# First loads in pieces and products of zeros, weight splits and context units at other places, in a two-layer kernel on one core

## The chip, the cores and the metric

The kernel runs on one core of a Trainium2 chip. Its time is the device time of one execution in microseconds (us), the median of the runs made. PE is TensorE, DVE is VectorE, ACT is ScalarE, POOL is GpSimd, and SP is SyncE, which here only starts transfers.

## What is computed

The input is `x`, 4 x 256 tokens of 256 values (1024 tokens in all), a context of the same shape, and integer token ids. Four blocks add to `x`, each scaled by the tanh of a gate:

```python
# layer 0: one of 4 gated experts, picked by token id, weights (4, 256, 256)
y = einsum(silu(h @ Wg[e].T) * (h @ Wu[e].T), Wd[e]);  out = where(expert_ids == e, y, out)
# layer 0: BitNet feed-forward, ternary weights, 8-bit tokens, Walsh-Hadamard transform before w_down
gate = bitlinear(x, w_gate); up = bitlinear(x, w_up)          # 256 -> 1024
out = h_bitlinear(silu(gate) * up, w_down)                    # act_quant(fwht(.)), 1024 -> 256
# layer 1: cross attention, 16 heads of 128; queries from tokens, keys and values from the context
scores = q @ k.T; out = (softmax(scores) @ v) @ Wo            # batches of 128 queries and 128 keys
# layer 1: 32 experts, top 8 in 2 of 4 groups, latent width 128, plus a shared expert
x = x + tanh(g) * block(layernorm(x))                         # around each of the four
```

`act_quant` takes the largest magnitude `am` of a token, rounds `x * 128 / am` and clips it to -128 .. 127. The layer norms have no weights.

## The kernel before

**Precision.** Weights and activations of the attention are float32. Each is split into a high part (a copy rounded to fp32r) and a low part (the rest), and a product is made of three passes of PE: `hi,lo`, `lo,hi` and `hi,hi` (L1540, L1541, L1542, called through `product`). A high part is written by ACT, a low part by DVE or POOL.

**Context units.** Keys and values of layer 1 come from the context alone, so PE makes them as filler work in units. A unit is six products 128x512 into one PSUM bank: the keys of one head (K) or the values of a group of four heads for one tile of tokens (V), for one half `g` of the tokens. There are 64 (`UNITS`, in the order of `BLOCKS`). `take` on ACT empties the bank, and SP stores the unit to DRAM. The table `FILLS` says how many of them stand at which named place ahead of the attention (`s0`, `s1`, `a11`, `y2`, `u0`, `f0`, ...: 26 in all, `FRONT_UNITS`); the rest stand one each at the places `m0`, `e0`, `m1`, `e1`, ... of the attention loop, m in the middle and e at the end of step u, except those that hold other tasks (`TASK_IN_STEP`).

**Weight blocks.** Weights arrive in 33 blocks of 128x1024 (`BLOCKS`: kind and head group, K, V, Q, O; S, D and E for the last block of the model). SP loads block j into `blk_raw[j % 2]`; `block_high(j)` on ACT (L820) writes the high part, `block_low(j)` on POOL (L574) the low part and counts `blk_done`. A unit of block j waits on PE for `blk_done >= j + 1`. In the attention loop these two calls are the last work of step u on ACT and on POOL, behind the key split of step u+2, for the block that `STEP_OF_BLOCK[u]` names: block 16 in step 7, block 18 in step 9. In the last part of the kernel the expert blocks are split at the units of `UNIT_OF_BLOCK` (ACT) and `LOW_UNIT_OF_BLOCK` (POOL).

**Order.** Each engine runs its own stream in the order of the code. The opening: SP loads context, block 0 and tokens; PE makes three units (`s0`), then transposes the normed tokens (`transpose_norm`, L1554). Then come the products of the four token-id experts for each half g (`a_sel`, masks `ge_row`), and the down products y0. `add_experts` on DVE adds a tile of y0 to `xr`. The BitNet part runs in steps n = 0 .. 7 through the tasks Q (transposes of the rounded tokens), G, U (gate and up), F (transposes of the `fly` product), H (Hadamard), D and C (L1725, L1734, L1740, L1750, L1757, L1763). POOL makes the first levels of the Hadamard transform (`fly`, `inner`, L626 to L632); `quantise` on DVE rounds tokens. Then the attention loop, 32 steps u (16 heads, two halves), and the expert part, 64 units i (32 experts, two halves).

**POOL ahead of the attention.** At the end of the BitNet part POOL runs `key_low(1)` (L580), then waits `h_ready`, then `block_low(7)`, `block_low(8)` and `block_low(9)`. DVE runs there the layer norm of the attention's tokens (L1088, L1089: two operations on 128x4) between operations that H(7) of PE waits for (L1376).

## Time and profile before

| | us |
|---|---|
| median of 3 runs (571.34, 569.83, 569.76) | 569.83 |
| the profiled execution | 570.37 |
| its span in the trace | 568.6 |
| PE busy | 538.2 (95%) |
| DVE, ACT, POOL busy | 389.0, 351.7, 319.9 |
| mean granted clock of TensorE | 0.990 of full |

The span is shorter than the time of the same execution by 1.8 us, which lies around it. A start in the rows below is in us from the span's start. A row of an engine in order of time has start, duration, engine, line of the kernel, operation, what is written from what, and in brackets the idle time ahead of it and who ended it.

### The profile page before, as it was taken

The numbers are of one execution on the slowest core, as the hardware profiler recorded it, in microseconds if no ns is written. First come the engines' busy times: TensorE is split into PE (matmuls) and PEld (weight loads), VectorE is DVE, ScalarE is ACT, GpSimd is POOL, SyncE is SP. The second block draws the span as 40 slices with busy tenths as digits, with TensorE's granted clock in tenths as the row PEclk, the third lists the DMA queues.
The fourth block names the chain that finished last, engine by engine and source line by source line (L and its number), as shares of the span: only waits on it lengthen the run. The fifth ranks groups of instructions, "written<-read, shape, count | busy, mean of one in ns | idle before, by whom it ended". The sixth has DMA issues, their size and how long they took to land.

```text
span 568.6 us, 9604 instructions
## 1 busy us (share of the span) xinstructions
PE 538.2 (95%) x3232; PEld 463.1 (81%) x3232; DVE 389.0 (68%) x818; ACT 351.7 (62%) x723; POOL 319.9 (56%) x318
## 2 busy tenths in 40 slices
PE   3999998998999999999999999999999979999997
PEld 3777766776878989999999999989998868777886
DVE  4867987589956576656655576646665766877882
ACT  3651144566488686766757565745757655777882
POOL 3579037899448797655544424426698464762320
PEclk9999998999999999999999999989999989999999
DMA  9901135610047768677696767534355734546761
GB/s 284 350 22 54 41 109 169 203 39 1 20 164 229 238 189 256 209 254 223 215 288 192 241 210 225 189 105 156 120 191 152 240 121 139 135 143 186 218 181 39
DMA packets 66673, 95.78 MB, mean 168 GB/s; under 512 B 6337, under 2 KB 38849, under 8 KB 66625
## 3 DMA queue, kind: packets, MB, share of 16 engines
q1 hardware_dynamic: 66624, 95.17, 53.6%
q8 instruction: 27, 0.44, 0.3%
q14 instruction: 22, 0.17, 0.1%
HBM read 67.23 MB, written 27.92 MB: 167 GB/s over the span
## 4 chain that ended last, share of the span: by engine, by line
PE 78%; DVE 7%; POOL 5%; ACT 4%; issue 2%; DMA 2%; SPq 0%; DVEq 0%; POOLq 0%; ACTq 0%
PE ps L1540 22%; PE ps L1541 21%; PE ps L1542 21%; PE ps L1645 4%; PE ps L1750 2%; PE ps L1734 2%; DMA xr<-in_x 1%; PE ps L1757 1%; ACT q2T L915 1%; PE ps L1763 1%; POOL kv_w_lo L574 1%; ACT kv_w_hi L820 1%; DMA k_hl<-k_scratch 1%; DVE xr L1194 1%; DVE a_sel L1180 1%
## 5 line engine op out<-in xcount | busy, mean ns | idle before, releaser
L651 POOL TENSOR_TENSOR probs<-probs,rsum 128x512 f32<-128x512 f32 x64 | 66.6, 1043 | 60.4 <-DVE rsum L1246 60.3
L1241 DVE TENSOR_REDUCE nmax<-ps 128x2 f32<-128x512 f32 x64 | 44.0, 688 | 35.6 <-PE ps L1542 35.3
L953 ACT ACTIVATE probs<-ps,nmax 128x256 f32<-128x256 f32 x128 | 59.8, 481 | 1.6 <-DVE nmax L1241 1.4
L1039 ACT ACTIVATE e_hi<-e_r 128x512 fp32r<-128x512 f32 x64 | 40.3, 630 | 31.5 <-DVE e_r L1466 30.4
L574 POOL TENSOR_TENSOR kv_w_lo<-blk_raw,kv_w_hi 128x1024 fp32r<-128x1024 f32 x16 | 38.9, 2434 | 36.2 <-ACT kv_w_hi L820 36.2
L1466 DVE SCALAR_TENSOR_TENSOR e_r<-ps,cw_row 128x512 f32<-128x512 f32 x64 | 43.5, 684 | 14.6 <-PE ps L1542 13.7
L1232 DVE TENSOR_TENSOR pT_lo<-ps,pT_hi 128x512 fp32r<-128x512 f32 x64 | 43.8, 685 | 11.8 <-ACT pT_hi L959 11.2
L1237 DVE TENSOR_TENSOR oT_lo<-ps,oT_hi 128x512 fp32r<-128x512 f32 x32 | 22.1, 692 | 40.1 <-ACT oT_hi L963 40.1
L774 POOL TENSOR_TENSOR e_lo<-e_sq,e_hi 128x512 fp32r<-128x512 f32 x19 | 24.6, 1294 | 43.2 <-ACT e_sq L1045 38.3
L959 ACT ACTIVATE pT_hi<-ps 128x512 fp32r<-128x512 f32 x64 | 38.3, 601 | 15.5 <-PE ps L1645 15.3
L963 ACT ACTIVATE oT_hi<-ps 128x512 fp32r<-128x512 f32 x32 | 19.1, 597 | 40.7 <-PE ps L1542 40.7
L580 POOL TENSOR_TENSOR k_hl<-k_hl 128x512 fp32r<-128x512 f32 x18 | 23.8, 1323 | 31.9 <-ACT k_hl L888 31.9
L1645 PE MATMUL ps<-eye,probs 128*128 128x128 f32 x256 | 39.0, 275 | 1.6 <-DVE kv_out L1272 0.9
L831 ACT ACTIVATE kv_hi<-ps 128x512 fp32r<-128x512 f32 x38 | 22.9, 603 | 26.9 <-PE ps L1542 26.9
L1540 PE MATMUL ps<-pT_hi,v_hl 128*128 128x256 f32 x128 | 36.7, 286 | 0.7 <-DVE pT_lo L1232 0.5
L1540 PE MATMUL ps<-k_hl,qT_lo 128*128 128x256 f32 x128 | 37.2, 291 | 0.0
L1542 PE MATMUL ps<-wo_hi,oT_hi 128*128 128x256 f32 x128 | 36.2, 283 | 0.0
L1541 PE MATMUL ps<-wo_lo,oT_hi 128*128 128x256 f32 x128 | 36.2, 283 | 0.0
L1540 PE MATMUL ps<-wo_hi,oT_lo 128*128 128x256 f32 x128 | 36.2, 283 | 0.0
L1542 PE MATMUL ps<-k_hl,qT_hi 128*128 128x256 f32 x128 | 36.2, 283 | 0.0
L1542 PE MATMUL ps<-pT_hi,v_hl 128*128 128x256 f32 x128 | 36.2, 282 | 0.0
L1541 PE MATMUL ps<-k_hl,qT_hi 128*128 128x256 f32 x128 | 36.1, 282 | 0.0
(292 smaller groups left out, 1873.1 us busy)
## 6 DMA issues: line engine op xcount, KB each, us to landing
cw_row<-cw_scratch SPq DMA_DIRECT2D x64, 256.0 KB, 3.7
v_hl<-v_scratch SPq DMA_DIRECT2D x24, 512.0 KB, 3.6
blk_raw<-in_w_blocks SPq DMA_DIRECT2D x23, 512.0 KB, 4.4
k_scratch<-kv_out SPq DMA_DIRECT2D x32, 256.0 KB, 2.7
v_scratch<-kv_out SPq DMA_DIRECT2D x32, 256.0 KB, 3.2
k_hl<-k_scratch SPq DMA_DIRECT2D x14, 512.0 KB, 3.5
v_scratch<-kv_hi SPq DMA_DIRECT2D x24, 256.0 KB, 2.7
blk_raw<-in_w_tail SPq DMA_DIRECT2D x10, 512.0 KB, 4.6
```

The source lines that it names most:

```text
L574: nc.gpsimd.tensor_tensor(lo[:, :], blk_raw[j % 2][:, :], hi[:, :].bitcast(F32), ALU.subtract).then_inc(blk_done, 1)
L651: nc.gpsimd.tensor_tensor(probs[:, b, :, :], probs[:, b, :, :], rsum[:, b, :].unsqueeze(2).to_broadcast([P, 2, S]), ALU.mult).then_inc(pro ...
L953: last = nc.scalar.activation(probs[:, b, t, :], ps[:, S_BANK[b], t * S:(t + 1) * S], ACT.Exp, bias=nmax[:, b, t:t + 1], accum_out=esum[:, ...
L959: nc.scalar.activation(pT_hi[:, b, :, :].rearrange("p k q -> p (k q)"), ps[:, P_BANK[b], :], ACT.Copy).then_inc(p_hi_done, 1)
L1039: nc.scalar.activation(e_hi[i % 4][:, :], e_r[i % 2][:, :], ACT.Square).then_inc(e_hi_done, 1)
L1232: V.tensor_tensor(pT_lo[:, b, :, :].rearrange("p k q -> p (k q)"), ps[:, P_BANK[b], :], pT_hi[:, b, :, :].rearrange("p k q -> p (k q)").bi ...
L1241: V.tensor_reduce(nmax[:, b, :], ps[:, S_BANK[b], :].rearrange("p (t k) -> p t k", t=2), AX.X, ALU.max, negate=True).then_inc(max_done, 1)
L1466: V.scalar_tensor_tensor(e_r[i % 2][:, :], ps[:, UP_BANK[i % 4], :], 0.0, cw_row[i % 4][:, :], ALU.max, ALU.mult).then_inc(root_done, 1)
L1540: mm(dst, l_lo, r_hi, start=first, stop=False, **kw)
L1541: mm(dst, l_hi, r_lo, start=False, stop=False, **kw)
L1542: return mm(dst, l_hi, r_hi, start=False, stop=last, **kw)
L1645: last = nc.tensor.transpose(ps[:, P_BANK[b], k * S + t * P:k * S + (t + 1) * P], probs[:, b, t, k * P:(k + 1) * P], ident)
```

## The change

1. **Opening.** The first transfers are cut: keys of the first head, context of half 0 in two chunks, the other keys, tokens, identity, the rest of the context. The units of block 0 have functions of their own: hi·hi first, then the two others as their parts arrive. `s0` holds 6 units, and `f1` 1 where it had 2. `FRONT_UNITS` is 28 where it was 26, and every later unit stands two places earlier. The low part of the second half of the context is made on POOL instead of DVE. Twelve products of zeros stand ahead of the first unit. SP stores the units of `s0` ahead of the weight loads for the BitNet part.
2. **Splits in front.** `block_high(1)` stands ahead of the token-id experts' silu, blocks 2, 3 and 4 a place earlier than before; `block_low(1)` ahead of the ternary rounding on POOL, and `block_low(2)`, `block_low(3)` no longer behind `scales_ready`. In `BLOCKS`, V2 and O0 change places (now 7 and 8). `block_low(7)` stands ahead of the wait for `h_ready`.
3. **Rounding.** The second half's four roundings go from DVE to ACT (`second_tokens`), `token_scales(1)` comes at i = 0 and `quantise(1)` at i = 1. The small operations of `quantise` are fewer. The transposes Q(0) wait for the takes one chunk at a time. `add_experts([0])` stands between two operations of the second half's z on DVE.
4. **Expert blocks.** Other units split them, and a table says at which unit they are loaded.

`STEP_OF_BLOCK` is as it was.

```diff
-        BLOCKS = [("K", 0), ("V", 0), ("K", 1), ("V", 1), ("K", 2), ("Q", 0), ("K", 3), ("O", 0), ("V", 2), ("Q", 1), ("V", 3),
+        BLOCKS = [("K", 0), ("V", 0), ("K", 1), ("V", 1), ("K", 2), ("Q", 0), ("K", 3), ("V", 2), ("O", 0), ("Q", 1), ("V", 3),
...
-        UNIT_OF_BLOCK = {0: 28, 4: 29, 6: 30, 9: 31, 10: 32}
-        LOW_UNIT_OF_BLOCK = {1: 28, 4: 29, 6: 30, 9: 31, 10: 32}
+        UNIT_OF_BLOCK = {0: 28, 6: 29, 7: 30, 10: 31, 16: 32}
+        LOW_UNIT_OF_BLOCK = {1: 28, 6: 29, 7: 30, 10: 31, 16: 32}
+        LOAD_AT_ROW = {4: 29, 8: 30, 13: 31, 16: 32}
...
-        FILLS = {"s0": 3, "s1": 1, "a11": 1, "y2": 1, "y6": 4, "u0": 2, "g1": 1, "u1": 3, "f0": 3, "g2": 1, "f1": 2, "d4": 0, "d5": 1, "c6": 1, "d6": 2}
+        FILLS = {"s0": 6, "s1": 1, "a11": 1, "y2": 1, "y6": 4, "u0": 2, "g1": 1, "u1": 3, "f0": 3, "g2": 1, "f1": 1, "d4": 0, "d5": 1, "c6": 1, "d6": 2}
...
-            load_context(0)
-            load_block(0)
+            sp.dma_start(blk_raw[0][:, 0:D], w_blocks[0, 0, :, 0:D]).then_inc(ld_keys[0], 16)
+            for c in range(DC):
+                sp.dma_start(cT_raw[:, c, 0:GT], ctx_t[c * P:(c + 1) * P, 0:GT]).then_inc(ld_ctx[c], 16)
+            sp.dma_start(blk_raw[0][:, D:4 * D], w_blocks[0, 0, :, D:4 * D]).then_inc(ld_keys[1], 16)
...
+            block_low(7)
             pool.wait_ge(h_ready, NG + 1)
-            block_low(7)
             block_low(8)
...
+            block_high(1)
             for g in range(NG):
                 if g:
                     first_expert(g)
                     take("a11")
-                    block_high(1)
+                    block_high(2)
...
+            def second_tokens():
+
+                take_unit(FILL_AT["u1"][0])
+                act.wait_ge(q1_scaled, 1)
+                act.wait_ge(q1T_filled, 1)
+                for n in range(GN, NT):
+                    last = nc.scalar.activation(qtok[:, n - GN, :], h[:, n, :], ACT.Copy, scale=am_r[:, n:n + 1], bias=ROUND)
+                last.then_inc(q1_rounded, 1)
+                for k in FILL_AT["u1"][1:]:
+                    take_unit(k)
...
+                if g:
+                    add_experts([0])
                 dve.wait_ge(z_hi_done, g + 1)
...
+            pe.wait_ge(zeros_ready, 1)
+            for _ in range(12):
+                mm(ps[:, 7, :], zeros[:, 0:P], zeros, start=True, stop=True)
             fill_units("s0")
```

**PE, the middle of attention step 8 (place m8).** Before: the scores of step 8, the transposed probabilities of step 7, and the third K1 unit of the second half. Its weights, `kv_w_*1`, are block 14.

```order
886 L1542 MATMUL ps<-k_hl0,qT_hi0 128x256
887 L1645 MATMUL ps<-eye,probs 128x128 x4
888 L1540 MATMUL ps<-cT_hi,kv_w_lo1 128x512
889 L1541 MATMUL ps<-cT_lo,kv_w_hi1 128x512
890 L1542 MATMUL ps<-cT_hi,kv_w_hi1 128x512
```

The same place now:

```order
875 L1584 MATMUL ps<-k_hl0,qT_hi0 128x256
876 L1706 MATMUL ps<-eye,probs 128x128 x4
877 L1582 MATMUL ps<-kv_w_hi0,cT_lo 128x512
878 L1583 MATMUL ps<-kv_w_lo0,cT_hi 128x512
879 L1584 MATMUL ps<-kv_w_hi0,cT_hi 128x512
```

The unit at m8 is now the first V1 unit, with the weights `kv_w_*0` of block 16, which before stood at m9. In the same way the first unit of block 18 moved from m12 to m10.

**POOL, the end of attention steps 6, 7 and 8.** Before, with what each row waits for:

```order
121 L651 TENSOR_TENSOR probs<-probs,rsum 128x512 [waits rsum_done]
122 L580 TENSOR_TENSOR k_hl1<-k_hl1 128x512 [waits k_hi_done]
123 L574 TENSOR_TENSOR kv_w_lo0<-blk_raw0,kv_w_hi0 128x1024 [waits blk_hi_done]
124 L651 TENSOR_TENSOR probs<-probs,rsum 128x512 [waits rsum_done] x2
125 L580 TENSOR_TENSOR k_hl0<-k_hl0 128x512 [waits k_hi_done]
```

Now:

```order
121 L662 TENSOR_TENSOR probs<-probs,rsum 128x512 [waits rsum_done]
122 L589 TENSOR_TENSOR k_hl1<-k_hl1 128x512 [waits k_hi_done]
123 L583 TENSOR_TENSOR kv_w_lo0<-blk_raw0,kv_w_hi0 128x1024 [waits blk_hi_done]
124 L662 TENSOR_TENSOR probs<-probs,rsum 128x512 [waits rsum_done] x2
125 L589 TENSOR_TENSOR k_hl0<-k_hl0 128x512 [waits k_hi_done]
```

The third row of both is the low part of block 16, in step 7: POOL's order here did not move, while PE's did.

**POOL, the end of the BitNet part.** Before (L580 is the key split of head 1, L574 the blocks 7, 8 and 9):

```order
L627 TENSOR_TENSOR fly<-inner 128x512
L631 TENSOR_TENSOR inner<-fly 128x2x256 [waits fly_step]
L632 TENSOR_TENSOR inner<-fly 128x2x256
L580 TENSOR_TENSOR k_hl<-k_hl 128x512 [waits k_hi_done]
L574 TENSOR_TENSOR wo_lo<-blk_raw,wo_hi 128x1024 [waits blk_hi_done,h_ready]
L574 TENSOR_TENSOR kv_w_lo<-blk_raw,kv_w_hi 128x1024 [waits blk_hi_done]
```

Now:

```order
L638 TENSOR_TENSOR fly<-inner 128x512
L642 TENSOR_TENSOR inner<-fly 128x2x256 [waits fly_step]
L643 TENSOR_TENSOR inner<-fly 128x2x256
L589 TENSOR_TENSOR k_hl<-k_hl 128x512 [waits k_hi_done]
L583 TENSOR_TENSOR kv_w_lo<-blk_raw,kv_w_hi 128x1024 [waits blk_hi_done]
L583 TENSOR_TENSOR wo_lo<-blk_raw,wo_hi 128x1024 [waits blk_hi_done,h_ready]
```

Block 7 (now V2) follows the key split directly; the wait for `h_ready` stands behind it.

## Rows read from the trace of the kernel before

**Rows 1.** The page, busy us of each engine with its share.

```profile
PE 538.2 (95%) x3232; PEld 463.1 (81%) x3232; DVE 389.0 (68%) x818; ACT 351.7 (62%) x723; POOL 319.9 (56%) x318
```

**Rows 2.** PE's waits: engine, line <- waited for: us, times, longest.

```profile
PE ps L1740 <- POOL inner L632: 2.1, 1, 2.1
PE ps L1540 <- DVE xr L1194: 1.8, 2, 1.1
...
PE ps L1725 <- ACT kv_out L829: 0.7, 1, 0.7
```

**Rows 3.** PE in order of time, the opening.

```profile
8.59 0.76 PE L1540 MATMUL ps<-cT_hi,kv_w_lo 128*128 128x512 f32 x1 [8.59 <-POOL kv_w_lo L591]
...
10.85 0.63 PE L1542 MATMUL ps<-cT_hi,kv_w_hi 128*128 128x512 f32 x1
11.28 0.49 PE L1540 MATMUL ps<-cT_hi,kv_w_lo 128*128 128x512 f32 x1
...
15.06 1.06 PE L1554 MATMUL ps<-eye,h 128*128 128x128 f32 x8 [0.77 <-DVE h L1107]
```

**Rows 4.** DVE in order of time, the opening.

```profile
8.09 1.41 DVE L1077 BATCH_NORM_STATS2 st<-xr 128x6 f32<-128x256 f32 x4 [0.50 <-DMA xr<-in_x]
...
12.75 2.17 DVE L1107 TENSOR_SCALAR h<-xr,mv,ln_y 128x256 f32<-128x256 f32 x4
```

**Rows 5.** Chain of waits around the first Hadamard step: start, us, what.

```profile
82.42 2.47 POOL kv_w_lo L574
```

**Rows 6.** PE in order of time, units at m8 and at m10.

```profile
236.20 0.48 PE L1540 MATMUL ps<-cT_hi,kv_w_lo 128*128 128x512 f32 x1
...
237.67 0.28 PE L1540 MATMUL ps<-k_hl,qT_lo 128*128 128x256 f32 x1
...
254.91 0.48 PE L1540 MATMUL ps<-kv_w_hi,cT_lo 128*128 128x512 f32 x1
```

**Rows 7.** ACT and POOL in order of time, end of steps 7 and 9.

```profile
235.33 0.60 ACT L831 ACTIVATE kv_hi<-ps 128x512 fp32r<-128x512 f32 x1 [1.51 <-PE ps L1542]
...
236.35 1.05 ACT L820 ACTIVATE kv_w_hi<-blk_raw 128x1024 fp32r<-128x1024 f32 x1
...
236.52 1.30 POOL L580 TENSOR_TENSOR k_hl<-k_hl 128x512 fp32r<-128x512 f32 x1 [1.96 <-ACT k_hl L888]
237.78 2.40 POOL L574 TENSOR_TENSOR kv_w_lo<-blk_raw,kv_w_hi 128x1024 fp32r<-128x1024 f32 x1
...
256.49 2.40 POOL L574 TENSOR_TENSOR kv_w_lo<-blk_raw,kv_w_hi 128x1024 fp32r<-128x1024 f32 x1
```

**Rows 8.** Stretches: us, busy (x) of PE, PEld, DVE, ACT, POOL, clock, DMA, GB/s.

```profile
90.00:93.40 3.40, 3.25 (x12) 2.99 (x13) 3.37 (x4) 1.03 (x1) 2.37 (x2) 0.50 0.28 102
462.06:465.50 3.44, 3.15 (x10) 2.70 (x11) 1.44 (x3) 2.67 (x5) 1.28 (x2) 0.50 0.95 323
```

**Rows 9.** POOL, DVE and PE in order of time, ahead of H(7).

```profile
144.35 1.28 POOL L580 TENSOR_TENSOR k_hl<-k_hl 128x512 fp32r<-128x512 f32 x1
...
144.45 1.20 DVE L1088 TENSOR_SCALAR ln_i<-ln_v 128x4 int32<-128x4 int32 x1
145.68 0.17 DVE L1089 TENSOR_SCALAR ln_y<-ln_i 128x4 int32<-128x4 int32 x1
...
148.43 1.22 DVE L1376 TENSOR_TENSOR fT_lo<-ps,fT_hi 128x1024 fp32r<-128x1024 f32 x1
...
149.75 0.47 PE L1750 MATMUL ps<-had,fT_lo 128*128 128x256 f32 x2 [0.85 <-ACT q L925]
```

**Rows 10.** POOL, DVE and PE in order of time, the expert part.

```profile
457.81 2.40 POOL L574 TENSOR_TENSOR kv_w_lo<-blk_raw,kv_w_hi 128x1024 fp32r<-128x1024 f32 x1
...
456.65 3.71 DVE L1265 TENSOR_SCALAR h<-xr,mv,ln_y 128x256 f32<-128x256 f32 x2 [2.26 <-POOL ln_y L666]
...
462.35 1.09 PE L1853 MATMUL ps<-eye,h 128*128 128x128 f32 x4 [3.80 <-DVE h L1265]
...
501.83 0.30 PE L1877 MATMUL ps<-eye,cw 128*128 128x128 f32 x1 [0.76 <-POOL cw L729]
```

More of the change, by code:

```diff
@@ L104, in flamingo_two_layer_kernel @@
         head_weights(1, early)
+        zeros = wq_hi[1][:, 0:512]
         region = ExitStack()
@@ L236, in flamingo_two_layer_kernel @@
         ld_blk = [sem(f"ld_blk{i}") for i in range(2)]
+        ld_keys = [sem(f"ld_keys{i}") for i in range(2)]
         ld_k = [sem(f"ld_k{i}") for i in range(2)]
@@ L833, in _, with context_high @@
[L833 to L839 removed]
+                    take_unit(k)
+            def context_high(c, g):
+                nc.scalar.activation(cT_hi[:, c, g * GT:(g + 1) * GT], cT_raw[:, c, g * GT:(g + 1) * GT], ACT.Copy).then_inc(ctx_hi_done, 1)
@@ new lines, in _ @@
+            act.wait_ge(ld_keys[0], 16)
+            nc.scalar.activation(kv_w_hi[0][:, 0:D], blk_raw[0][:, 0:D], ACT.Copy).then_inc(first_keys_hi_done, 1)
+            for c in range(DC):
+                act.wait_ge(ld_ctx[c], 16)
+                context_high(c, 0)
+            act.wait_ge(ld_keys[1], 16)
+            nc.scalar.activation(kv_w_hi[0][:, D:4 * D], blk_raw[0][:, D:4 * D], ACT.Copy).then_inc(first_keys_hi_done, 1)
+            for k in FILL_AT["s0"]:
+                if k == 2:
+                    act.wait_ge(ld_ctx[2], 16)
+                    for c in range(DC):
+                        context_high(c, 1)
+                take_unit(k)
@@ L1219, in quantise @@
-                own(last)
+                    dve.wait_ge(q1_rounded, 1)
+                else:
+                    own(token_scales(0))
+                    for n in range(GN):
+                        last = V.tensor_scalar(qtok[:, n, :], h[:, n, :], am_r[:, n:n + 1], ROUND, ALU.mult, ALU.add)
+                    own(last)
                 V.tensor_scalar(qtok[:, :, :], qtok[:, :, :], ROUND + 127.0, ROUND - 128.0, ALU.min, ALU.max).then_inc(q1_ready, 1)
-                own(V.tensor_scalar(am_c[:, s], am[:, s], 1.0 / 128.0, None, ALU.mult))
@@ L1335, in step_task_low @@
                     shared_relu(n, bank)
-            for n in range(GN):
-                add_experts([n], n - 1 if n else None)
+            for n in range(1, GN):
+                add_experts([n], n - 1)
             dve.wait_ge(y0_taken, GN)
@@ L1557, in transpose_norm, with first_keys @@
                 last.then_inc(hT_filled, 1)
+            def first_keys(k, n, g):
+                tokens = slice(g * GT, (g + 1) * GT)
+                at = [slice((n * DC + c) * P, (n * DC + c + 1) * P) for c in range(DC)]
+                pe.wait_ge(first_keys_hi_done, 1 if n == 0 else 2)
+                for c in range(DC):
+                    pe.wait_ge(ctx_hi_done, g * DC + c + 1)
+                    mm(ps[:, fill_bank(k), :], kv_w_hi[0][:, at[c]], cT_hi[:, c, tokens], start=(c == 0), stop=False)
+                if n == 3:
+                    pe.wait_ge(blk_done, 1)
+                else:
+                    pe.wait_ge(first_keys_done, n + 1)
+                for c in range(DC):
+                    mm(ps[:, fill_bank(k), :], kv_w_lo[0][:, at[c]], cT_hi[:, c, tokens], start=False, stop=False)
+                for c in range(DC):
+                    pe.wait_ge(ctx_late_done if g else ctx_done, c + 1)
+                    last = mm(ps[:, fill_bank(k), :], kv_w_hi[0][:, at[c]], cT_lo[:, c, tokens], start=False, stop=(c == DC - 1))
+                return last
             def fill_units(key):
```

179 lines of the change are left out of this document (90 added, 89 removed).

## The prediction

> **What bounds the kernel now.** I read the page's busy times first, then what PE waits for, then PE in order of time around each wait. PE is busy 538.2 of 568.6 us [rows 1]; no other engine passes 68%. Span less busy time leaves PE 30.4 us, the tail behind its last product included, and 8.6 of them are the start [rows 3]. So two things move the time: work that leaves PE, or waits that go or come on PE. Whatever the other engines gain counts only where PE waits for them, and the longest such waits behind the start are few: 3.8 us in the expert part [rows 10], 2.1 us ahead of the first F, 1.8 us in two waits for `xr` [rows 2]. The reader should also see which waits are not there: no row says that PE waits for a `kv_w_lo` of L574. Every weight block is ready when its first unit comes.
>
> The sum is made against the profiled execution, 570.37 us. The median is 569.83, 0.54 below it, and I carry the difference over to the median.
>
> **Opening.** Three more units stand ahead of the token transposes. A unit costs PE 1.4 us: six products from 236.20 to 237.67 with the first start-up in it [rows 6]. The transposes start at 15.06 because `h` is written from 12.75 on for 2.17 us, and DVE could begin on the tokens at 8.09, when they landed [rows 3, 4]. The tokens stand in the SP queue behind the same bytes as before, cut into more pieces. So 15.06 stays, if six units fit before it. Before, the first product waited until 8.59 for the low part of the keys; now the hi·hi products need only the high parts, about 1 us earlier, and six units at 1.4 are 8.4 us: 7.6 + 8.4 = 16.0 when the clock is full, hidden but for 0.9, and tokens that land as much earlier would give it back. Bounds: -0.5 (tokens a little earlier) to +2 (units at the low clock). I take 0. The twelve products of zeros lie in time in which PE had nothing to do: nothing on the path. What they may change is the rate: products ran 0.43 us apart until 11.28, where the next starts come at half that [rows 3]. That row shows the rate rising after 2.7 us of products and not what zeros do. Against that rule, at the low rate three more units would cost 3 x 1.4 more, which is beyond my upper bound only if the tokens wait for all of it.
>
> **From there to Q(1), -3.0.** (a) `add_experts([0])` moves forward, so the first y0 bank is free in time: the longer of the two waits for `xr`, 1.1, goes [rows 2]. (b) One more ACT copy of 1.05 us (the price of L820, [rows 7]) stands ahead of the experts' silu, and the first expert's copy of the second half comes behind it: 0 to +1.05; ACT had little slack there, I take +0.85. (c) Q(0) goes chunk by chunk: of its wait of 0.7 [rows 2] two thirds go, -0.45. (d) F(0) waits 2.1 for POOL's `inner` [rows 2], and ahead of POOL's four `fly` operations stood a block split of 2.47 us at 82.42 [rows 5]. It comes earlier now. With the split gone, what sets the start is the DVE product that `fly` reads, which was done shortly before POOL's split ended at 84.9; I take it that the chain starts up to 1.65 sooner: -1.65, and with the whole wait gone -2.1. (e) `f1` has a unit less, 1.4 us of PE work; but Q(1) now waits for ACT, which has four roundings more, so I take half: -0.65. Sum -1.1 + 0.85 - 0.45 - 1.65 - 0.65 = -3.0. Bounds -3.95 (b costs nothing) to -1.5 (c and e give nothing and d half).
>
> A fall of the granted clock to 0.50 (1.2 of 2.4 GHz) follows the 2.1 us wait, from 90.0 to 93.4 [rows 8]. If (d) comes true it may not happen: up to 1.6 more. I leave that in the range.
>
> **Attention loop, two units fewer, -2.8.** The units that left are whole PE work, 2 x 1.4. PE is busy without a gap there, so it counts in full.
>
> **Attention loop, two new waits, +8.1.** `STEP_OF_BLOCK` is unchanged, but each unit comes two places sooner. Block 16 is split at the end of step 7 and now wanted at m8; block 18 at the end of step 9 and wanted at m10. Before they were wanted at m9 and m12. PE reached m8 at 236.20 and m10 at 254.91 [rows 6]. POOL ended the low part of block 16 at 237.78 + 2.40 = 240.18, that of block 18 at 256.49 + 2.40 = 258.89 [rows 7]. PE waits 4.0 us in both, and with the step from POOL's end to PE's start 4.05: 8.1. This can't come earlier by itself: on ACT the split stands behind the take of the unit e7 (235.33, [rows 7]), which waits for PE, and on POOL behind the key split that begins at 236.52. Without that key split POOL could begin at 236.35 + 1.05 = 237.40, so the floor is 3.6 each. Of all other blocks the first unit comes at least one step behind the split, some 5 us of slack. PE is the bound of the loop, so nothing gives the 8.1 back: the steps behind are moved as a whole. What is queued behind the waiting product is all of PE: probabilities times values, output projection, and with them ACT and DVE.
>
> **Clock after the waits, +2.8.** After PE's idle 2.1 us and 3.8 us the clock stood at 0.50 for 3.4 us each time [rows 8, 10]. A wait of 4.05 us is longer than both. A stretch of 3.44 us at half rate costs at most 1.7 us; around 462.35 some of it is idle, and I take 1.4 for each. Bounds 0 to 3.4.
>
> **Block 7, +2.2.** `block_low(7)` no longer waits for `h_ready`; it begins when the key split ends, 144.35 + 1.28, less a little overlap, 145.6. DVE's L1088, an operation on 128x4, took 1.20 us beside that key split, its twin L1089 0.17 us [rows 9]: DVE was held until POOL's operation ended. L1089 began at 145.68, so a POOL operation of 2.40 us begun at 145.6 would hold it until 148.0, 2.15 later than its old end. All of DVE's chain to `fT_lo` (148.43) follows, and PE waits for it already (0.85 at 149.75, [rows 9]). So +2.2; if DVE comes first it is 0, if more DVE operations meet it +3.9. The Trainium skill (SBUF — State Buffer, "Who interferes with whom") calls the port pair that the two engines share an exclusive lock which whoever starts first keeps for the whole instruction. By that rule the term is all or nothing, 2.2 or 0, decided by less than 0.1 us; the row agrees in that the small operation ended with POOL's.
>
> **Expert part, +0.4.** PE's wait of 3.8 at 462.35 is for two `h` operations of DVE that took 3.71 us beside POOL's low part of a block (457.81, 2.40) [rows 10]. That block is now split two units later, so about 1.7 goes (to 3.4 if all). But the last block's split now stands at unit 16, on POOL ahead of the chain to `cw`, for which PE waits 0.76 at 501.83 [rows 10]: 2.4 more in that chain less 0.3 of slack is +2.1 (0 to +3.5 with the clock). Sum -1.7 + 2.1.
>
> **Small things, 0.** Two heads more are stored raw, so ACT and POOL split two keys more (POOL 1.30 each, [rows 7]) in the loop, where POOL is at 56% and none is waited for. Second context low parts on POOL: ahead of masks that have time.
>
> **Sum.** 0 - 3.0 - 2.8 + 8.1 + 2.8 + 2.2 + 0.4 = +7.7. From 570.37 that is 578.1; from the median **577.5 us**.
>
> **Rivals.**
> (A) The two waits are gone: **566.6, chance 0.06, the other side.** The splits of blocks 16 and 18 would be ready as PE comes. Then 8.1 and 2.8 drop out: 577.5 - 10.9. It decides at 3.2 us: while the two waits with their clock falls together stay under 10.9 - 7.7 = 3.2 us the kernel is not slower. For it speaks only that ACT and POOL have idle time in each step; against it, that both splits stand behind work which PE itself releases less than 1 us before [rows 7].
> (B) Waits as above, but no clock falls and DVE comes first at block 7: 577.5 - 2.8 - 2.2 = **572.5, chance 0.17.** For it: the 0.1 us that decides, and that the 90 us fall may go.
> (C) More goes wrong at the edges: tail +3.5 in place of 0.4 and a further fall of the clock behind the H wait, +1.6: **582.2, chance 0.13.**
> (D) The opening gives nothing: zeros don't raise the clock, the six units run over 15.06 by 2, and (e) gives nothing: **580.2, chance 0.10.**
> (E) The change doesn't do what it says in front: F(0) still waits for POOL, because DVE and not the block split set its start (d = 0 in place of -1.65): 579.2, within the main case's spread.
>
> **How the numbers follow.** Main case (with E) 0.54, its own spread 575 to 580. A change of under 0.3% (1.7 us) can't be told from none; A is faster by more than that, and a piece of B's lower edge reaches it. Faster 0.07, same 0.04, slower 0.89. The range leaves out A and a part of C: 571.5 to 582.5.
>
> **What would show it.** PE's waits should hold a new row, the first product of a unit waiting for `kv_w_lo` of POOL's block split, two times of about 4 us, near 232 and 250; the granted clock should stand at 0.50 behind each. A POOL block split should overlap a small operation of the layer norm of 2 us ahead of H(7). The wait for `xr` should be down to one, F(0) under 1 us. PE's count grows by 12, and its idle total by some 8 us. The forecast is wrong if the waits at m8 and m10 are under 2 us, or if the front gains more than 6 us.

## The result, and the profile after

The changed kernel takes **582.28 us** in the median of six runs (579.79 to 584.13), against 569.96 us of the kernel before beside it (569.45 to 573.03). The ratio is 1.0199, with a 95% interval of 1.0179 to 1.0219: it is slower by 2%. The profiled execution took 580.26 us, with a span of 578.4 us and a mean granted clock of 0.985.

The first view is the page of the changed kernel, its busy times; it answers to [rows 1].

```profile
span 578.4 us, 9631 instructions
...
PE 546.3 (94%) x3244; PEld 469.3 (81%) x3244; DVE 383.6 (66%) x809; ACT 354.7 (61%) x732; POOL 325.2 (56%) x322
```

PE has 12 instructions more, the products of zeros. Its busy time grew by 8.1 us. Of these, 5.5 are the zeros, which stand in time where PE had been idle. I put the rest down to the lower clock (0.985 against 0.990). The second view is what PE waits for, as in [rows 2] (engine, line <- waited for: us, times, longest).

```profile
PE ps L1582 <- POOL kv_w_lo L583: 7.4, 2, 3.7
PE ps L1812 <- ACT q L964: 3.1, 1, 3.1
PE ps L1596 <- DVE h L1146: 2.7, 1, 2.7
PE ps L1918 <- DVE h L1305: 1.8, 1, 1.8
PE ps L1802 <- POOL inner L643: 1.7, 1, 1.7
...
PE ps L1787 <- issue: 1.4, 1, 1.4
```

The first row has no counterpart before: two waits for the low part of a block. The second stands ahead of H(7), the third at the tokens' transposes in the opening. The wait for `h` in the expert part fell from 3.8 to 1.8. The next view, PE in order of time, shows the first three rows at their four places:

```profile
18.45 1.94 PE L1596 MATMUL ps<-eye,h 128*128 128x128 f32 x8 [2.67 <-DVE h L1146]
...
152.39 0.48 PE L1812 MATMUL ps<-had,fT_lo 128*128 128x256 f32 x2 [3.11 <-ACT q L964]
...
242.55 0.50 PE L1582 MATMUL ps<-kv_w_hi,cT_lo 128*128 128x512 f32 x1 [3.70 <-POOL kv_w_lo L583]
266.80 0.60 PE L1582 MATMUL ps<-cT_hi,kv_w_lo 128*128 128x512 f32 x1 [3.71 <-POOL kv_w_lo L583]
```

and POOL at the two block splits (start, us):

```profile
238.93 1.27 POOL L589 TENSOR_TENSOR k_hl<-k_hl 128x512 fp32r<-128x512 f32 x1 [1.96 <-ACT k_hl L924]
240.16 2.34 POOL L583 TENSOR_TENSOR kv_w_lo<-blk_raw,kv_w_hi 128x1024 fp32r<-128x1024 f32 x1
...
264.41 2.35 POOL L583 TENSOR_TENSOR kv_w_lo<-blk_raw,kv_w_hi 128x1024 fp32r<-128x1024 f32 x1
```

240.16 + 2.34 = 242.50, and PE starts at 242.55. The wait ahead of H(7) is put down to ACT's `q`, but that was done at 151.6. The product reads `fT_lo`, which DVE writes until 152.28, and it starts at 152.39:

```profile
151.06 1.22 DVE L1418 TENSOR_TENSOR fT_lo<-ps,fT_hi 128x1024 fp32r<-128x1024 f32 x1
```

The stretches of low clock of the changed kernel, up to the end of PE's work, have the columns of [rows 8]. The first three start within or just behind one of PE's waits, the other two behind no wait at all:

```profile
17.89:21.30 3.41, 2.85 (x11) 2.69 (x12) 2.17 (x7) 1.20 (x2) 3.33 (x2) 0.50 1.03 413
243.17:246.58 3.41, 3.41 (x14) 3.03 (x13) 0.27 (x1) 0.60 (x1) 0.00 (x0) 0.50 0.18 66
267.06:270.47 3.41, 3.41 (x12) 2.85 (x12) 0.00 (x0) 0.60 (x1) 0.00 (x0) 0.50 0.41 134
386.53:389.94 3.41, 3.41 (x16) 3.31 (x16) 0.69 (x1) 0.72 (x2) 0.00 (x0) 0.50 0.03 10
...
482.10:485.51 3.41, 3.41 (x10) 2.64 (x9) 1.14 (x2) 1.56 (x4) 2.54 (x2) 0.50 0.77 256
```

One such fall of the clock, 3.41 us at half rate, takes 0.003 from the mean granted clock of an execution. So the mean clocks can be read as a count. The profiled execution (0.985) has the five falls above, and the six executions of the changed kernel, 0.979 to 0.988, have four to seven. Where two traces can be laid side by side, a fall costs 1.2 to 1.8 us. A straight line through the six times against their clocks gives 1.2 us a fall. I use 1.2 to 1.8 as an estimate below.

The table shows where the time went: by how much later each place comes than in the kernel before (starts from both traces).

| place | before | after | later by |
|---|---|---|---|
| tokens' transposes | 15.06 | 18.45 | 3.4 |
| Q(1) | 106.24 | 106.67 | 0.4 |
| H(7) | 149.75 | 152.39 | 2.6 |
| first product at m8 | 236.20 | 242.55 | 6.4 |
| first product at m10 | 254.91 | 266.80 | 11.9 |
| transposes of `h`, expert part | 462.35 | 471.14 | 8.8 |
| transposes of `cw` | 501.83 | 511.08 | 9.3 |
| end of the span | 568.6 | 578.4 | 9.8 |

### The profile page after: what moved, and what is told of

It reads as the page before. It is cut to its first block, busy times and chain, and to the rows that moved or that the text cites. A ratio compares the mean times of both kernels' runs of the same rounds, so it can differ in the third digit from the quotient of the medians.

```text
span 578.4 us, 9631 instructions
## 1 busy us (share of the span) xinstructions
PE 546.3 (94%) x3244; PEld 469.3 (81%) x3244; DVE 383.6 (66%) x809; ACT 354.7 (61%) x732; POOL 325.2 (56%) x322
## 4 chain that ended last, share of the span: by engine, by line
PE 75%; DVE 8%; POOL 7%; ACT 4%; issue 3%; DMA 3%; SPq 0%; DVEq 0%; POOLq 0%
PE ps L1582 21%; PE ps L1583 20%; PE ps L1584 20%; PE ps L1706 4%; PE ps L1812 2%; PE ps L1796 2%; PE ps L1819 1%; DMA xr<-in_x 1%; DMA cw_row<-cw_scratch 1%; ACT q2T L954 1%; PE ps L1825 1%; POOL kv_w_lo L583 1%; DVE st L1116 1%; DVE h L1146 1%; DVE e_r L1508 1%
## 5 line engine op out<-in xcount | busy, mean ns | idle before, releaser
L589 POOL TENSOR_TENSOR k_hl<-k_hl 128x512 fp32r<-128x512 f32 x20 | 26.4, 1318 | 37.3 <-ACT k_hl L924 37.3
L841 ACT ACTIVATE kv_hi<-ps 128x512 fp32r<-128x512 f32 x36 | 21.7, 602 | 33.3 <-PE ps L1584 33.3
L1582 PE MATMUL ps<-pT_hi,v_hl 128*128 128x256 f32 x128 | 36.6, 286 | 0.7 <-DVE pT_lo L1272 0.5
L1583 PE MATMUL ps<-k_hl,qT_hi 128*128 128x256 f32 x128 | 36.9, 289 | 0.0
L1584 PE MATMUL ps<-k_hl,qT_hi 128*128 128x256 f32 x128 | 36.9, 288 | 0.0
L839 ACT ACTIVATE kv_out<-ps 128x512 f32<-128x512 f32 x28 | 16.7, 597 | 32.5 <-PE ps L1584 26.6
```

What stands on the lines that cost most here:

```text
L1582: mm(dst, l_lo, r_hi, start=first, stop=False, **kw)
L1583: mm(dst, l_hi, r_lo, start=False, stop=False, **kw)
L1584: return mm(dst, l_hi, r_hi, start=False, stop=last, **kw)
```

## The experiments

All edits are to the changed kernel unless said otherwise. The kernel before was run beside each group: 570.6 us with both experiments on the steps, block 7 behind `h_ready` and the late context; 571.05 with the same edit on the kernel before, the three together, the old units and the first run with one product of zeros; 570.22 with the rest. The changed kernel itself was run only beside 569.96 us. "Less than the changed kernel" below therefore compares medians of different groups, whose kernel before differs by up to 1.1 us.

**Blocks 16 to 18 a step earlier.** This takes PE's reason to wait away and leaves everything else.

```diff
-        STEP_OF_BLOCK = {0: 10, 1: 11, 2: 12, 3: 13, 4: 14, 5: 15, 7: 16, 8: 17, 9: 18, 11: 19, 12: 20, 13: 21, 15: 22,
+        STEP_OF_BLOCK = {0: 10, 1: 11, 2: 12, 3: 13, 4: 14, 5: 15, 6: 16, 7: 17, 8: 18, 11: 19, 12: 20, 13: 21, 15: 22,
```

> The changed kernel with blocks 16, 17 and 18 split at the ends of steps 6, 7 and 8 instead of 7, 8 and 9; nothing else. Theory (two waits): PE's two waits of 3.70 and 3.71 us for the low part of a block are gone, and with them the two falls of the granted clock at 243.2 and 267.1, worth 1.7 to 1.8 us each: 582.3 - 7.4 - 3.5 = 571.4 us, still above the kernel before by about 1.5. Rival (other engines follow: the waits only showed what ACT and POOL lack in those steps): the waits go, but others come in their place, and the time falls by under 4 us, to 578 or more. Second rival: the clock falls stay without the waits: 574.9.

Measured: 569.94 us (567.58 to 571.51), ratio to the kernel before 0.9988 (0.9971 to 1.0004). That is 12.3 us less than the changed kernel, against 10.9 expected. PE's waits of this kernel:

```profile
PE ps L1812 <- ACT q L964: 3.1, 1, 3.1
PE ps L1596 <- DVE h L1146: 3.0, 1, 3.0
PE ps L1582 <- DVE e_lo L1518: 2.2, 3, 1.3
PE ps L1918 <- DVE h L1305: 1.8, 1, 1.8
```

The row of `kv_w_lo` is gone. The waits for `q` and for both `h` stayed as they were. In the expert part the waits for `e_lo` grew from 1.1 to 2.2 us in all and the one for `s_sq` from 0.9 to 1.4; the fall at 482.1 is not in this trace, so PE gets there sooner. Both falls of the clock in the loop's middle went too, and one came behind H(7), at 153.2. Other engines did not take the place of the two waits in the loop, so the first rival falls; the clock went with the waits, so the second does.

**Block 16 alone.** Blocks 17 and 18 stay where they are.

```diff
-        STEP_OF_BLOCK = {0: 10, 1: 11, 2: 12, 3: 13, 4: 14, 5: 15, 7: 16, 8: 17, 9: 18, 11: 19, 12: 20, 13: 21, 15: 22,
+        STEP_OF_BLOCK = {0: 10, 1: 11, 2: 12, 3: 13, 4: 14, 5: 15, 6: 16, 8: 17, 9: 18, 11: 19, 12: 20, 13: 21, 15: 22,
```

> The changed kernel with only block 16 split a step earlier (end of step 6); block 18 stays at the end of step 9. Theory (each wait by itself costs its own length and one fall of the clock): the wait at m8 and its fall go, the wait at m10 stays at 3.7 us with its fall: 582.3 - 3.7 - 1.8 = 576.8 us. Rival (the second wait is a consequence of the first, the engines being out of step): both go or the second shrinks below 2 us: 574 or less.

Measured: 576.26 us (574.86 to 580.1), 1.0125 (1.0086 to 1.0164), where 576.8 was expected. The trace has one wait of 3.71 us at m10, so the second wait is no consequence of the first. The first is worth 6.0 us by these medians and the second 6.3, about half of the 12.3 us each.

**The block ahead of the key.** In steps 7 and 9 the block's split goes ahead of the key's on both engines. The lines for POOL are shown; those for ACT, with `block_high` and `key_high`, are of the same form.

```diff
+                if u in (7, 9):
+                    block_low(STEP_OF_BLOCK[u])
                 key_low(u + 2)
...
-                if u in STEP_OF_BLOCK:
+                if u in STEP_OF_BLOCK and u not in (7, 9):
                     block_low(STEP_OF_BLOCK[u])
```

> The changed kernel with one thing in another order: in steps 7 and 9 the split of the block stands ahead of the split of the key, on ACT and on POOL. Theory (the split starts when PE has made the unit before it, and the wait is what remains of ACT's 1.05 and POOL's 2.4 us behind that): ACT's copy begins 0.5 us sooner, POOL's operation 0.9 us sooner, and PE's two waits are 2.8 us each in place of 3.7: 582.3 - 1.8 = 580.5 us, or 1.7 to 3.5 us less again if a wait of 2.8 us draws no fall of the clock. Rival (the waits are set by something else, the load of the block or the stores): they stay at 3.7.

Measured: 577.01 us (576.16 to 578.25), 1.0123 (1.0098 to 1.0147). POOL and PE at m8:

```profile
241.19 2.35 POOL L583 TENSOR_TENSOR kv_w_lo<-blk_raw,kv_w_hi 128x1024 fp32r<-128x1024 f32 x1 [2.39 <-ACT kv_w_hi L833]
...
243.59 0.50 PE L1586 MATMUL ps<-kv_w_hi,cT_lo 128*128 128x512 f32 x1 [2.91 <-POOL kv_w_lo L583]
```

Both waits are 2.9 us, where 2.8 was expected: their length is what is left of ACT's and POOL's work behind the unit before. They fell by 0.8 each, 1.6 in all, and the time fell by 5.3. In this profile the clock fell at 244.88 behind the first wait and not behind the second, and the falls at 386.5 and 482.1 did not come either. The mean granted clock of its four runs is 0.9888 against 0.9835 in the changed kernel, which is 1.8 falls fewer a run, or 2.2 to 3.2 us by the estimate. That leaves 0.5 to 1.5 us of the 5.3 open.

**Block 7 behind `h_ready` again.**

```diff
-            block_low(7)
             pool.wait_ge(h_ready, NG + 1)
+            block_low(7)
```

> The changed kernel with the low part of block 7 behind the wait for h_ready again, as before. Theory (POOL's split held DVE's small operation): the operation on 128x4 ahead of H(7) takes 0.2 us instead of 2.30, PE's wait ahead of H(7) falls from 3.11 to about 0.9: -2.2, 580.1 us. Rival (H(7) is late for DVE's own work, or the block is then late for m0): the wait of 3.11 stays or one of 2 us appears at m0, 582.3 us.

Measured: 578.1 us (575.7 to 579.18), 1.0129 (1.0101 to 1.0157), 4.2 us less than the changed kernel. PE's wait ahead of H(7) is 0.92 us, as expected. DVE's small operation of the norm, in the changed kernel and here:

```profile
144.97 1.20 DVE L1127 TENSOR_SCALAR ln_i<-ln_v 128x4 int32<-128x4 int32 x1
146.20 2.30 DVE L1128 TENSOR_SCALAR ln_y<-ln_i 128x4 int32<-128x4 int32 x1
```

```profile
145.46 1.20 DVE L1127 TENSOR_SCALAR ln_i<-ln_v 128x4 int32<-128x4 int32 x1
146.70 0.17 DVE L1128 TENSOR_SCALAR ln_y<-ln_i 128x4 int32<-128x4 int32 x1
```

2.30 us against 0.17 for the same four elements a partition: POOL's operation (146.10, 2.37 us) began 0.1 us sooner, and DVE's ended with it. The rule that the prediction drew from the Trainium skill (SBUF — State Buffer, "Who interferes with whom"), all or nothing by who starts first, agrees with these two rows. The 2.0 us beyond the expected 2.2 are of the size of the clock's falls: the mean granted clock of these four runs is 0.987 against 0.9835, 1.2 falls fewer a run, or 1.4 to 2.2 us by the estimate. Which falls they are stays open. In the profile of the changed kernel none follows the 3.1 us wait, but one does in those of the experiment with earlier steps (153.2), with the block ahead of the key (152.7) and with the late context on DVE (149.5). The profile of this experiment lacks the falls at 386.5 and 482.1 instead, which no wait draws.

**The same edit on the kernel before.** There `block_low(7)` is put ahead of the wait, the reverse of the diff above.

> The kernel before with one edit: the low part of block 7 stands ahead of the wait for h_ready, as in the change. Theory (POOL's operation of 2.4 us holds DVE's operation on 128x4): the operation takes 2.3 us, PE's wait ahead of H(7) grows from 0.85 to 3.1: +2.2 us, 572.4 against 570.2, and up to 1.7 more where the clock falls behind that wait. Rival (in the kernel before there is slack, the wait being shared with other causes): within 0.5 us of the kernel before.

Measured: 573.57 us (572.75 to 574.88) against 571.05, ratio 1.0049 (1.0035 to 1.0062): +2.5 us. PE and the clock behind it:

```profile
150.85 0.76 PE L1750 MATMUL ps<-had,fT_lo 128*128 128x256 f32 x2 [3.02 <-ACT q L925]
```

```profile
149.78:156.60 6.82, 5.75 (x26) 5.68 (x27) 6.41 (x19) 1.02 (x3) 0.00 (x0) 0.50 0.11 41
```

One line moved gives back the pattern in another kernel: DVE's operation takes 2.29 us, the wait is 3.02 in place of 0.85, and a fall begins in it that lasts twice as long as any in the kernel before. This profile also lacks the falls at 90 and 376.7 that the profile of the kernel before has, and has another at 477.5, so the 2.5 us can't be split into wait and clock.

**The late context on DVE.** The two low parts go from POOL to DVE, between the factors of the first norm and its tokens.

```diff
-            for c in range(DC):
-                pool.wait_ge(ctx_hi_done, DC + c + 1)
-                nc.gpsimd.tensor_tensor(cT_lo[:, c, GT:T], cT_raw[:, c, GT:T], cT_hi[:, c, GT:T].bitcast(F32), ALU.subtract)\
-                    .then_inc(ctx_late_done, 1)
...
-            norm(0).then_inc(h_ready, 1)
+            for n in range(GN):
+                last = stats(n)
+            own(last)
+            factors(0, GN)
+            for c in range(DC):
+                dve.wait_ge(ctx_hi_done, DC + c + 1)
+                V.tensor_tensor(cT_lo[:, c, GT:T], cT_raw[:, c, GT:T], cT_hi[:, c, GT:T].bitcast(F32), ALU.subtract).then_inc(ctx_late_done, 1)
+            scaled(0).then_inc(h_ready, 1)
```

> The changed kernel with the low parts of the late context made by DVE, between the factors and the tokens of the first norm (two operations of 0.69 us), instead of by POOL. Theory (POOL's two operations of 1.27 held DVE's small ones at 11.38 and 12.64, 1.2 us each in place of 0.16, and pushed POOL's masks into the rest): the factors end at 12.5, the tokens' transposes start at 16.5 instead of 18.45 and the fall of the clock at 17.9 goes, worth 1.6: -3.5, 578.8 us. Rival (the tokens are held by the masks and by six units): the transposes start no earlier than 18 and the fall stays: 582.3 us.

Measured: 578.47 us (575.27 to 579.1), 1.013 (1.0099 to 1.0162), 3.8 us less than the changed kernel. In the changed kernel, POOL and then DVE in the opening:

```profile
11.29 2.55 POOL L604 TENSOR_TENSOR cT_lo<-cT_raw,cT_hi 128x512 fp32r<-128x512 f32 x2 [1.37 <-ACT cT_hi L849]
13.93 8.49 POOL L608 TENSOR_SCALAR ge_row<-ids_row 128x1024 int32<-128x1024 int32 x3
```

```profile
11.38 1.23 DVE L1134 SCALAR_TENSOR_TENSOR ln_t<-ln_y 128x4 f32<-128x4 f32 x1
12.64 1.22 DVE L1135 TENSOR_TENSOR ln_t<-ln_t,ln_v 128x4 f32<-128x4 f32 x1
...
14.09 0.89 DVE L1134 SCALAR_TENSOR_TENSOR ln_t<-ln_y 128x4 f32<-128x4 f32 x1
```

In the experiment all of these take 0.16 or 0.17, and the transposes start at 16.97:

```profile
12.54 0.17 DVE L1132 SCALAR_TENSOR_TENSOR ln_y<-ln_t,ln_y 128x4 f32<-128x4 f32 x1
12.74 1.29 DVE L1170 TENSOR_TENSOR cT_lo<-cT_raw,cT_hi 128x512 fp32r<-128x512 f32 x2
13.95 2.87 DVE L1142 TENSOR_SCALAR h<-xr,mv,ln_y 128x256 f32<-128x256 f32 x4
```

DVE does more work itself and the transposes still start 1.5 us sooner. The `h` operations still take 2.87 for four beside POOL's masks, 2.17 in [rows 4]. The fall at 17.9 is gone. The rival, by which the transposes start no earlier than 18 and the fall stays, falls. The 3.8 us are met in part by chance. In the profile the gain has grown to 2.8 us at Q(1) (103.91 against 106.67), and then a fall behind H(7), at 149.5, takes 1.5 of it back.

**The three together.** The earlier steps, block 7 behind `h_ready` and the late context on DVE.

> The changed kernel with three of its parts undone or mended: blocks 16 to 18 split a step earlier, the low part of block 7 behind h_ready, the late context's low parts on DVE between the factors and the tokens. Theory (the costs are separate and the rest of the change is a gain): 569.9 (steps alone) less 2.2 ahead of H(7), less 3.5 in the opening: 564.2 us, 1.1% under the kernel before. Rival (a cost goes and the next one takes its place, or the falls of the clock come elsewhere): 567 us or more.

Measured: 563.85 us (562.07 to 564.44), 0.9871 (0.9855 to 0.9887); once more, in the last group, 563.47 us, 0.9879 (0.9856 to 0.9902). It is 18.4 us faster than the changed kernel and 1.3% faster than the kernel before. The costs are separate: one by one they give 12.3 + 4.2 + 3.8 = 20.3, and together 18.4. The profile with earlier steps lacks the fall at 482.1 and that with block 7 both falls that no wait draws, while the profile of the three has both (370.1 and 465.7). So the 20.3 is somewhat too high.

**The expert blocks at their old units**, on top of the three.

```diff
-        UNIT_OF_BLOCK = {0: 28, 6: 29, 7: 30, 10: 31, 16: 32}
-        LOW_UNIT_OF_BLOCK = {1: 28, 6: 29, 7: 30, 10: 31, 16: 32}
-        LOAD_AT_ROW = {4: 29, 8: 30, 13: 31, 16: 32}
+        UNIT_OF_BLOCK = {0: 28, 4: 29, 6: 30, 9: 31, 10: 32}
+        LOW_UNIT_OF_BLOCK = {1: 28, 4: 29, 6: 30, 9: 31, 10: 32}
+        LOAD_AT_ROW = {4: 29, 8: 30, 10: 31, 13: 32}
```

> The same as the kernel with three parts mended, and the expert blocks split and loaded at the units of the kernel before. Theory (the new units save 2.0 us of PE's wait for h and give part of it back in front of cw, where the last block's split stands in POOL's chain): this one is 0.5 to 1.5 us slower than the three together, 565.2 us, with a wait of 3.8 us for h and one fall of the clock behind it. Rival (my forecast for the tail, +0.4 for the new units): this one is 0.4 us faster, 563.8.

Measured: 566.5 us (563.82 to 566.86), 0.9916 (0.9899 to 0.9932), 2.65 us more than the three beside it. PE in the expert part, old units and then new:

```profile
456.71 1.08 PE L1921 MATMUL ps<-eye,h 128*128 128x128 f32 x4 [3.77 <-DVE h L1308]
```

```profile
454.61 0.63 PE L1921 MATMUL ps<-eye,h 128*128 128x128 f32 x4 [1.75 <-DVE h L1308]
...
485.88 0.50 PE L1585 MATMUL ps<-hT_hi,kv_w_lo 128*128 128x512 f32 x1 [0.92 <-DVE s_sq L1334]
492.08 0.50 PE L1585 MATMUL ps<-e_hi,wo_lo 128*128 128x512 f32 x1 [0.42 <-DVE e_lo L1521]
494.48 0.30 PE L1945 MATMUL ps<-eye,cw 128*128 128x128 f32 x1 [0.74 <-POOL cw L736]
```

The new units save 2.0 us at `h` and give 1.3 back in two small waits ahead of `cw`. A fall of the clock is not the rest: the old units have one behind the 3.77 us wait (456.3), but the new ones have one too, at 465.7. What the old units have besides are two waits that the trace with the new ones lacks:

```profile
475.08 0.50 PE L1585 MATMUL ps<-hT_hi,kv_w_lo 128*128 128x512 f32 x1 [0.77 <-DVE xl_lo L1325]
...
532.44 0.50 PE L1585 MATMUL ps<-e_hi,wq_lo 128*128 128x512 f32 x1 [0.73 <-DVE e_lo L1521]
```

2.0 + 0.8 + 0.7 - 1.3 = 2.2 of the 2.65 us. The rival, 0.4 us the other way, falls.

**One product of zeros for twelve**, on top of the three.

```diff
-            for _ in range(12):
-                mm(ps[:, 7, :], zeros[:, 0:P], zeros, start=True, stop=True)
+            mm(ps[:, 7, :], zeros[:, 0:P], zeros, start=True, stop=True)
```

> The same as the kernel with three parts mended, with one product of zeros in place of twelve; the other eleven are left out and nothing that is computed changes. Theory (the products of zeros bring the rise of the clock ahead of the units): the first units run 0.43 us a product instead of 0.23 for some 3 us, the six units end 1.4 us later, at about 17.2 and so behind the tokens; the transposes start 0.3 to 1 us later: 564.8 us against 564.2. Rival (zeros cost or gain nothing because the tokens decide): equal within 0.3 us. Second rival (without them the clock stays low until the tokens): 2 us or more slower.

Measured: 562.55 us (562.11 to 562.93), 0.9852 (0.9838 to 0.9866), where 564.8 was expected. The first of the six units run at the low rate, and still the transposes lose only 0.56 us (16.81 to 17.37). The pairs of products of one kernel with one product of zeros, in order of time:

```profile
9.84 1.06 PE L1617 MATMUL ps<-cT_hi,kv_w_lo 128*128 128x512 f32 x2
...
11.54 0.95 PE L1611 MATMUL ps<-cT_hi,kv_w_hi 128*128 128x512 f32 x2
12.33 0.63 PE L1617 MATMUL ps<-cT_hi,kv_w_lo 128*128 128x512 f32 x2
```

and with twelve:

```profile
5.88 0.88 PE L1611 MATMUL ps<-cT_hi,kv_w_hi 128*128 128x512 f32 x2
6.60 0.62 PE L1617 MATMUL ps<-cT_hi,kv_w_lo 128*128 128x512 f32 x2
```

So with twelve zeros the full rate comes with the second pair of real products, and with one only with the last pair shown. This agrees with the rule that the prediction drew from the Trainium skill (TensorE: Matmul & The Clock Gate, Part 1: The HAM clock gate). But the higher rate was hardly needed: with one product of zeros the six units end at 17.37, 0.3 us behind the tokens' last `h` (17.09). Since the median was 1.3 us lower and not higher, both were run again beside each other:

> The kernel with three parts mended once more, beside the one without zeros. Theory (both are the same but for 0.6 us in the opening; the 1.3 us between their medians came from falls of the clock that a run has or has not): within 1 us of each other, 563.3. Rival (zeros cost something behind the opening, the clock falls come with them): this one again 1.3 us slower, 563.9 against 562.6.

> The kernel with three parts mended and one product of zeros in place of twelve, once more; eleven products of zeros are left out. Theory: within 1 us of the one with zeros, about 563.5, slower if anything by the 0.6 us of its opening. Rival: 562.6 again, the zeros cost 1.3 us.

Measured: 563.47 us with zeros and 562.32 us without, ratios 0.9879 (0.9856 to 0.9902) and 0.9878 (0.9849 to 0.9907). The intervals cover each other. The transposes of this pair start at 17.76 with zeros and 16.80 without, so even the 0.56 us was no fixed cost. In both profiles with twelve zeros the clock falls once near 370 in the middle of the kernel, and in both with one it doesn't, at the same products. By the mean granted clocks of all twenty runs there are 1.3 falls a run with zeros (ten runs, clock 0.9960) and 0.8 without (0.9975). By the estimate that is 0.6 to 0.9 us of the 1.2 to 1.3 between the medians. The products of zeros gain nothing that these runs can show. Whether they draw falls, or the difference is chance, stays open.

**The first addition late again**, on top of the three.

```diff
-                if g:
-                    add_experts([0])
                 dve.wait_ge(z_hi_done, g + 1)
...
-            for n in range(1, GN):
-                add_experts([n], n - 1)
+            for n in range(GN):
+                add_experts([n], n - 1 if n else None)
```

> The kernel with three parts mended, with add_experts([0]) again behind the last product of the second half's z, as before the change. Theory (the early addition frees the y0 bank, one of the change's gains): PE's wait of 1.1 us for xr comes back and the time is 1.1 us more than with the three parts mended, 565.0 against 563.9. Rival (ACT's copies set that place anyway): no difference.

Measured: 561.93 us (560.75 to 562.51), 0.9853 (0.9832 to 0.9874), 1.5 us less than the three in the same group where 1.1 more was expected. No wait for `xr` came back. So the longer wait of [rows 2] for `xr` did not go because the addition moved, and the theory of the expectation is wrong. The kernel before shows why it was there, DVE's product of z and POOL beside it:

```profile
45.63 3.27 DVE L1180 TENSOR_TENSOR a_sel<-a_sel,a_silu 128x1024 f32<-128x1024 f32 x1 [1.20 <-ACT a_silu L871]
```

```profile
45.42 2.40 POOL L574 TENSOR_TENSOR kv_w_lo<-blk_raw,kv_w_hi 128x1024 fp32r<-128x1024 f32 x1
```

The same product takes 1.23 in the changed kernel, where `block_low(1)` comes ahead of the ternary rounding and no longer stands beside it. From the product's start to the first addition DVE takes 6.12 us before (45.63 to 51.75) and 3.98 in this run (46.65 to 50.63), 2.1 less. That this is why the wait went is read from the rows; no run puts `block_low(1)` alone back. The forecast was wrong in the cause. In the later position the addition is no slower. The median with it is the lowest that was run, but its profile lacks the fall near 370 as those with one product of zeros do. Its first four `h` operations also take 2.10 us in place of 2.87: POOL's masks begin at 14.09, behind the first of them (13.85), and not ahead of it. So the 1.5 us are no proof of a gain.

## Why the prediction was right, step by step

The direction and the main cause hold: two waits for a block split, with falls of the clock behind them, and a small DVE operation held ahead of H(7). The forecast 577.5 was 4.8 us low. That 582.28 lies inside the range, by 0.2 us, is luck: two terms were wrong and partly cancel, and the cost that was missing was not thought of. Rival C names nearly this time (582.2), but not for its reason, since the expert part didn't lose 3.5 us. The terms, in the order of the sum:

- **Opening, 0 (to +2): wrong, +3.4.** The step that failed is "second context low parts on POOL: ahead of masks that have time", which I had put among the small things. I asked only who waits for POOL's result. The cost is on DVE: while POOL made the late context and began its masks, three small operations of the norm took 1.23, 1.22 and 0.89 us in place of 0.16 each, 2.9 us more. The `h` operations took 0.7 more beside the masks. So the token transposes moved from 15.06 to 18.45. PE's wait of 2.67 there drew a fall of the clock (17.9), which the sum did not have either. The experiment with the late context on DVE takes the held operations and the fall away. It gives back 1.5 of the 3.4, since DVE then makes the low parts itself (1.3) and the `h` operations stay slow. The six units end at 15.78 in the changed kernel, so 0.7 of the 3.4 would stand even with the tokens in time. The very rows that carried the term of block 7 [rows 9] would have told it here too.
- **To Q(1), -3.0: right in the sum, wrong in its parts.** From the transposes to Q(1) it is 91.18 us before and 88.22 after, -2.96. But the fall of the clock at 90 [rows 8] is in the first, and most of the one at 17.9 is in the second. With the three edits together, where no fall stands in this stretch, it is 16.81 to 103.78, 86.97: 4.2 less than before, of which up to 1.7 are the fall before (half of 3.41), so about -2.5 without it. Its parts: (a) the wait of 1.1 went, by another cause; (b) +0.85 did not come, no wait is there; (c) -0.44; (d) the wait for `inner` went from 2.1 to 1.7, -0.4 where I took -1.65; (e) the unit less of 1.4 and a wait ahead of Q(1) that grew from 0.73 to 1.43, -0.7. Together -2.6. In (d) the block split was not what held the chain, which is rival E; it was counted to the main case. The bounds of this term were also summed wrongly: with (b) at nothing it is -3.85, and with (c) and (e) at nothing and half of (d) it is -1.1, not -1.5.
- **Two units fewer, -2.8:** it holds as a sum. From H(7) to PE's wait of 0.6 us for `probs` late in the loop it is 263.2 us before (149.75 to 412.94) and 260.1 with the three edits (147.23 to 407.28), -3.1, with one fall in both. They leave behind m10 and not ahead of m8, since each place up to there still holds a unit. So the two waits came at 242.55 and 266.80 and not near 232 and 250: without the 2.8, and with the opening's 3.4, PE arrives at 236.20 + 3.4 - 3.0 + 2.3 = 238.9, as measured.
- **Two waits, +8.1: +7.41.** POOL's start moved with PE's, as expected. Rival A, the other side, is excluded by the trace; the experiment with earlier steps is what A would have needed, and it stands at 0.9988.
- **Clock behind them, +2.8:** two falls at 243.2 and 267.1. From the arrival at m8 to the one at m10, PE took 24.24 us (238.85 to 263.09); without the wait of 3.70 that is 20.54, against 18.71 of the kernel before (236.20 to 254.91): 1.8 us for the first fall, where I had taken 1.4. The experiment with earlier steps gives 12.3 us for the two waits and their falls, where 7.4 + 2 x 1.8 is 11.0.
- **Block 7, +2.2: +2.26** (3.11 less 0.85), and a fall behind it in some profiles but not in that of the changed kernel; rival C had it as 1.6.
- **Expert part, +0.4: wrong, -1.0 between these two traces and -2.65 by the experiment.** The wait for `h` fell by 2.0 (I had -1.7). The +2.1 for `cw` did not come. POOL's chain did grow as I said: from the start of `wsel` to the end of `cw` it takes 11.58 us before (490.11 to 501.69) and 13.72 after (497.22 to 510.94). But PE comes later too, held by two waits of 0.95 and 0.44 for DVE, and its wait for `cw` stays 0.77. From the transposes of `h` to the end the changed kernel takes 1.0 us more (9.8 less 8.8 in the table), so with the 2.0 it is -1.0.

The terms that were too low (opening +3.4, clock +0.8) and too high (waits 0.7, expert part 1.4) leave about +2 net for the profiled execution; its 580.26 is 2.2 over my 578.1. The remaining 2 us lie between that execution and the median. By the mean granted clock the profiled execution has five falls, and two of the three executions above 582.5 us have six (0.982) and the third seven (0.979). One more fall is 1.2 to 1.8 of the 2.0. Where in the kernel it stands is in no trace; behind the wait ahead of H(7) would be one place.

Of the signs that I had named, the new row of waits, the low clock behind both, the held operation ahead of H(7), the single wait for `xr` and the 12 instructions came. Two did not: F(0) still waits 1.71 us and not under 1, and PE's idle time grew from 30.4 to 32.1 us, not by 8. The zeros fill 5.5 us of what was idle; without them it would be 7.2.

## What to carry to other kernels

When units move in a table, move the table of their suppliers with them. Here a split that ended one step ahead was free. The same split at the end of the step just before its first use made PE wait for what was left of the copies on ACT and POOL, 3.7 us, plus what the clock took. When work goes to POOL, ask which small DVE operations run beside it, not only who waits for the result: an operation on four elements a partition lasted 2.3 us beside a POOL operation of 2.4. Give each part of a bundle its own run, since here a bundle that was 2% slower held one 1.3% faster than the kernel before. And before a difference of 1 or 2 us is explained by the edit, compare the mean granted clocks of the runs.
